# Graph layer and expert layer on one core: GpSimd's edge-row gathers may run four groups ahead of the segment sums in place of two

## The reference, cut to what matters

```python
def _L0_gnn_ref(feat, W_self, W_neigh, b, src, dst):
    msg = feat[src]                                          # 100000 rows of 256
    agg = jax.ops.segment_sum(msg, dst, num_segments=n)      # summed by destination
    deg = jax.ops.segment_sum(jnp.ones_like(dst, dtype=feat.dtype), dst, num_segments=n)
    h_neigh = agg / jnp.maximum(deg, 1.0)[:, None]
    return feat @ W_self + h_neigh @ W_neigh + b

# _L0_ffn_ref: layer norm, router logits, top 2 of 8 experts, softmax of the two, and
    for e in range(E):
        h = jax.nn.gelu(jnp.einsum('bsd,dh->bsh', xn, W1[e]) + b1[e], approximate=False)
        y_e = jnp.einsum('bsh,hd->bsd', h, W2[e]) + b2[e]
        y = y + y_e * w_full[..., e, None]

x = x + _L0_gnn_ref(_layernorm(x), ...)
x = x + _L0_ffn_ref(_layernorm(x)[None], ...)[0]
```

## Time and profile before

| | us |
|---|---|
| median of three runs | 1377.52 |
| the profiled execution | 1373.36 |
| its span, from first to last instruction | 1371.5 |
| TensorE matmuls busy | 1122.6 (82%) |
| VectorE busy | 861.0 (63%) |
| ScalarE busy | 427.6 (31%) |
| GpSimd busy | 948.0 (69%) |

### The profile page before, as it was taken

How to read it: one execution, slowest core, us unless ns; L and a number is a source line. 1 busy time by engine, 2 the same in 40 slices (tenths; PEclk the granted TensorE clock), 3 DMA queues, 4 the chain that set the end, 5 groups by cost and what they waited for, 6 DMA issues and landing times.

```text
span 1371.5 us, 22195 instructions
## 1 busy us (share of the span) xinstructions
PE 1122.6 (82%) x6356; PEld 990.3 (72%) x6357; DVE 861.0 (63%) x2801; ACT 427.6 (31%) x804; POOL 948.0 (69%) x1027
## 2 busy tenths in 40 slices
PE   0357888987996788999888888788798898989977
PEld 0246777887885687898777677677687786877867
DVE  6765565657576475776667567576476765655537
ACT  5612232323242233344233334232333331311221
POOL 5746575767676677676676677677777777777774
PEclk9888999999998899999999999999899999999999
DMA  9778797875545447566654655564577677766766
GB/s 332 254 247 258 241 286 235 266 251 173 181 151 182 141 141 233 180 228 193 192 183 147 197 174 179 177 186 141 187 229 244 211 230 211 247 217 222 226 194 220
DMA packets 174489, 287.57 MB, mean 210 GB/s; under 512 B 25632, under 2 KB 105888, under 8 KB 174240
## 3 DMA queue, kind: packets, MB, share of 16 engines
q1 hardware_dynamic: 123232, 153.76, 34.3%
q0 software_dynamic: 45696, 124.88, 30.2%
q10 hardware_dynamic: 5440, 7.47, 1.6%
HBM read 228.81 MB, written 57.20 MB: 209 GB/s over the span
## 4 chain that ended last, share of the span: by engine, by line
PE 67%; DVE 13%; issue 12%; POOL 3%; DMA 3%; DVEq 1%; SPq 1%; ACT 0%; POOLq 0%; ACTq 0%
PE bank L965 23%; PE bank L1041 16%; PE bank L1067 10%; PE bank L1075 6%; PE bank L953 3%; PE bank L994 3%; PE bank L996 3%; POOL ring L690 2%; DVE agg L1312 2%; DVE heap L1469 1%; DVE onehot L1258 1%; PE bank L1091 1%; DMA heap<-in_x 1%; PE bank L1102 1%; PE bank L1011 1%
## 5 line engine op out<-in xcount | busy, mean ns | idle before, releaser
L690 POOL DMA_INDIRECT ring<-feature_table,src_sb x760 | 742.9, 977 | 342.4 <-issue 204.9
L965 PE MATMUL bank<-ring,onehot 128*128 128x257 f32 x1552 | 412.4, 412 | 186.2 <-issue 126.9
L965 PEld LDWEIGHTS bank<-ring,onehot 128*128 128x128 f32 x1552 | 311.5, 205 | 253.4 <-issue 196.8
L1312 DVE SCALAR_TENSOR_TENSOR agg<-bank,in_first,agg 128x257 f32 x196 | 94.5, 482 | 186.4 <-PE bank L965 122.8
L867 ACT ACTIVATE heap<-heap 128x512 f32<-128x512 f32 x139 | 87.6, 630 | 350.3 <-DVE heap L1469 350.3
L1469 DVE TENSOR_TENSOR heap<-bank,b_sb 128x512 f32<-128x512 f32 x139 | 95.9, 690 | 154.8 <-PE bank L1041 81.2
L1067 PE MATMUL bank<-heap 128*128 x728 | 181.7, 394 | 12.5 <-DVE y_out L1478 6.6
L1041 PE MATMUL bank<-row_t,heap 128*128 128x128 f32 x1456 | 183.2, 281 | 0.6 <-DVE heap L1469 0.6
L1041 PEld LDWEIGHTS bank<-row_t,heap 128*128 128x128 f32 x1456 | 178.1, 198 | 2.2 <-issue 0.8
L1067 PEld LDWEIGHTS bank<-heap 128*128 128x128 f32 x728 | 137.2, 196 | 30.5 <-issue 13.4
L1258 DVE TENSOR_TENSOR onehot<-iota,target 128x512 f32<-128x512 f32 x196 | 134.4, 686 | 7.0 <-DVE xf L1329 5.4
(11 more groups left out here) (190 smaller groups left out, 1269.5 us busy)
## 6 DMA issues: line engine op xcount, KB each, us to landing
heap<-in_w SPq DMA_DIRECT2D x139, 512.0 KB
expert_out<-empty_row SPq DMA_DIRECT2D x68, 256.0 KB
ring<-feature_table,src_sb POOLq DMA_INDIRECT x760
row<-expert_rows SPq DMA_DIRECT2D x91, 128.5 KB, 4.3
xf<-in_x SPq DMA_DIRECT2D x49, 128.0 KB
ff<-feature_table SPq DMA_DIRECT2D x49, 128.0 KB
expert_out<-inside SPq DMA_DIRECT2D x46, 128.0 KB
expert_out<-y_out SPq DMA_DIRECT2D x45, 128.0 KB
```

The source lines that it names most:

```text
L690: pool.indirect_dma_start(group_row(t, i)[:, 0:D], None, x if t < RAW else table, bass.IndirectOffsetOnAxis(src_sb[:, k:k + 1], 0)).then_i ...
L965: last = pe.matmul(bank[t % 2][:, 0:D + 1], onehot[:, q, i, :], group_row(t, i), start=(i == 0), stop=(i == GT - 1))
L1312: last = dve.scalar_tensor_tensor(out=a, in0=bank[t % 2][:, 0:D + 1], scalar=mask[:, g:g + 1], in1=a, op0=ALU.mult, op1=ALU.add)
```

## The change

One constant, which is read in one place, the wait of `gather` at line 685. From group 10 on a gather waits for the matmuls of group t - 4 in place of those of group t - 2. Nothing else is changed: not the ring, not the number of dense blocks (six, before and after), and no other engine's program.

```diff
-ROWS_AHEAD = 2
+ROWS_AHEAD = 4
```

## The result

The changed kernel takes 1282.82 us in the median of four runs (1278.36 to 1287.98), the kernel before 1378.74 beside it: a ratio of 0.9303, interval 0.9263 to 0.9343. That is 95.9 us less by the medians (91 to 102 by the interval of the ratio); 88 to 89 us less and 1289 us were forecast.

A forecast was written before the change was run, and what follows sets the result against it. TensorE and GpSimd waiting for each other bound the kernel, with GpSimd's own work limiting the gain. Stretches summed to 84.6 us, the books gave 88 to 100; 88 was taken: 1377.5 - 88, forecast 1289 us, range 1266 to 1330.

The forecast's parts named there:

- The loop of two: Gathers of group t wait for sums of t - 2, those sums for gathers: GpSimd stands 136.2 us, TensorE 126.9.
- The smaller of two waits, by stretches: In five stretches, the smaller of TensorE's wait for gathers and GpSimd's wait for sums counts as gain: 84.6 us.
- 300 to 500 us: Second stretch: TensorE waits 24.7 us, GpSimd has 22.9 to give above its spacing; 22.9 us counts.
- 700 to 1000 us: Fourth stretch: TensorE waits 44.4 us, GpSimd has 16.7 to give above its spacing; 16.7 us counts.
- The last term: Stretch from 1000 to 1320 us: TensorE waits 18.3 us, GpSimd has 5.6 to give; 5.6 us counts.
- the bound of 104.4: GpSimd's total wait for sums above spacing, the gain in us if the cushion carried without limit between stretches.
- the group-by-group books: Gather and matmul starts recomputed per group with the trace's durations and landings: four groups give 88 to 100 us less.
- Costs put at nothing: Clock gives back up to some 20 us on TensorE, mostly waiting; scatters taken at 2 us; merges covered; tail unchanged.
- The rule on shared queues: Gathers share DMA engines with weight loads and land later; with every landing at 5 us the sum hardly moves.
- Another wait that takes half the gain: Rival: TensorE then stands for VectorE's one-hots or PSUM banks; half of 88 us lost, 1333 us, chance 0.10.
- GpSimd was not slowed either: Rival: GpSimd's gathers lengthen through SBUF contention with VectorE; mean gather 1138 ns gives 1408 us, chance 0.05.
- What the profile after was to show: TensorE's issue idle 40 to 65 us, GpSimd's waits 20 to 50, TensorE's share 86% or more, clock above 0.95.

The follow-up runs named there:

- The copies: A 256 KB HBM-to-HBM copy on ScalarE's queue in each of 186 slots: kernel before 1405.24 us, changed kernel 1281.76 us.
- the 46 gathers: In every fourth group from 12 on, a plain copy on ScalarE's queue replaces the fourth gather: kernel before 1346.99 us, changed kernel 1241.91 us.

## Why the prediction was right, point by point

**The loop of two.** That the idle time without a releaser is the landing of gathered rows, and that GpSimd was let go too late, was right. At 60 groups of the trace before, TensorE's wait ends 0.09 us after the last of the group's rows has landed; these waits are 135.3 us together. The copies show it from the side: 0.44 us of later landing cost 30 us with two groups, and 0.51 us cost nothing that can be measured with four.

**The smaller of two waits, by stretches.** The sum of 84.6 us met the profiled pair's 85.4 us, and four of the five terms were right within 2 us. Part of that is luck. The pair sets a fast execution of before against the slowest of the changed kernel; between the medians it is 95.9 us, and the interval, 91 to 102, leaves out the sum and the 88 us that were taken. And the step counted each stretch for itself, while GpSimd's lead (from the first gather's issue to the group's first matmul) is carried over the borders. Counted in the two timelines, the first gather of groups 40, 71, 102, 147 and 195 was issued 36.8, 48.8, 62.5, 78.4 and 86.6 us earlier. From group 40 to 71 (300 to 500 us) GpSimd itself thus gained 12.0 us, not the 22.9 that were to count, since it still stood 8.8 us there and its operations took 2.5 us longer; TensorE's 21.1 us came about because 9 us of lead from the start were spent (19.7 us at group 40 against 9.6 before, 10.0 at group 71 against 9.0). That term was met by two errors that cancel.

The one that was plainly mis-sized is 700 to 1000 us: 22.6 in place of 16.7. GpSimd's own gain, 15.9 us, was as forecast, but it comes there with a lead. The first gather of group 102 was issued, in the kernel before and in the changed one, at

```profile
690.11 0.99 POOL L690 DMA_INDIRECT ring<-feature_table,src_sb  x1 [1.27 <-PE bank L965]
```

```profile
627.58 0.99 POOL L690 DMA_INDIRECT ring<-feature_table,src_sb  x1 [0.30 <-issue]
```

and TensorE began the group's matmuls 7.05 us later before (697.16) and 12.34 us later after (639.92). The 5.3 us more were carried over the border at 700 us and spent behind it (at group 147 the lead is 1.5 us shorter than before), which is nearly the 5.9 us that the term lacked. The last term, 5.6 us, was met exactly, though 18.3 us of TensorE's waits stood there: GpSimd had nothing to give. The measured 95.9 us of the medians lies between the sum by stretches and the bound of 104.4, inside the group-by-group books (88 to 100). Taking 88, the low end, for VectorE's lags was too careful by some 8 us.

**Costs put at nothing.** Scatters: the idle time before the changed kernel's 84 scatters at line 698 is the spacing, none is longer than 0.32 us; the 2 us taken for them was not needed. The clock gave back 24 us of TensorE's busy time, against "up to some 20". The sums of group 61 before and of group 143 after ran at a granted clock of 0.50, that is 1.2 GHz, after 6.88 and 4.31 us of idle time; 17 groups took over 3 us before and 12 after. That most of the 24 us passes as waiting fits the idle time, which fell by 61.5 us and not by 84.6, but no run changes the clock alone, so it is not shown. The tail kept its length within 0.1 us. At the start 7.8 us of the first wait stayed, where about 6 were taken.

**The rule on shared queues.** The copies on ScalarE's queue made the gathers' landings later by 0.44 and 0.51 us. The Trainium skill, page DMA: Bandwidth & Descriptors, section SWDGE vs HWDGE vs iDMA, has GpSimd's transfers and the others take turns in the same engines. The later landings agree with that, though no run shows the turns themselves. The run-ahead alone hardly moved the landings: the mean was 3.08 us with two groups and 3.11 with four, the median 2.74 and 3.02.

**The rivals.** Another wait that takes half the gain did not come: VectorE's one-hots hold TensorE 6.9 us in the changed kernel, 8.3 before, and taking work off GpSimd still brings 41 us. GpSimd was not slowed either, with 4 ns on the mean gather where 120 would have turned the sign. VectorE's share rose from 63% to 67% meanwhile. The Trainium skill, GPSIMD Engine Reference, section Key points, has GpSimd contend for SBUF with VectorE's instructions that have two SBUF inputs; no run here sets such contention apart, and the mean gather shows no growth of it.

**What the profile after was to show.** All within the bounds given but TensorE's share: 85%, where "86 or more" stood.

**What stays open.** By the books taking off the 46 gathers should have brought 18 us before the change, and it brought 30. Shorter landings aren't the cause: the mean was 3.10 us with those gathers off and 3.08 with them. Nor is it known why the medians differ by 10 us more than the profiled pair.

## What to carry to other kernels

When two engines wait for each other around a buffer, take both waits by stretches of the run and add up the smaller of the two: that is roughly what more run-ahead can give. Where one is used up it gives nothing, except what a lead gained earlier still carries over the border. Before deepening a queue, look whether the buffer already has the room; here the first added group brought seven eighths or more of the gain. Once the standing is gone, the producer's own work is the time of the kernel: here each us taken off GpSimd brought 0.7 us, and each us added cost 0.9 (in the kernel before, with its standing, about half a us either way).

## What the runs showed of the hardware

A GpSimd clear of 0.33 us behind an indirect DMA begins as that DMA ends and lies partly in the 0.30 us that otherwise pass before the next DMA: one clear cost 0.19 us, two cost 0.81. So the 0.30 us between GpSimd's DMAs took up only 0.14 of the 0.33 us of the first clear, and the second clear, which also waits for a semaphore of the first, cost 0.62 us more, over three times as much. Whether that semaphore is the reason was not tried apart.
